# Four of eight ternary weight pieces moved from ScalarE and VectorE to GpSimd

## The reference

```python
def step(carry, xs):                    # 128 of these, one after the other
    r, state = carry
    qt, kt, vt = xs
    r = decay * r + kt * vt
    retained = (qt * r).reshape(B, D)
    inp = retained @ Wi.T + bi
    gate = sigmoid(inp @ Wg.T + bg)
    blended = gate * state + (1.0 - gate) * inp
    state = tanh(blended @ A.T + inp @ Bm.T)
    return (r, state), state @ Wo.T + bo

def _quantize(W):                       # W1 is 1024 x 256, W2 is 256 x 1024
    gamma = mean(abs(W))
    return clip(round(W / (gamma + EPS)), -1.0, 1.0)

x = x + tanh(g_xattn) * mixer(layernorm(x), ctx)
h = relu(layernorm(x) @ _quantize(W1).T + b1)
x = x + tanh(g_ffn) * (h @ _quantize(W2).T + b2)
```

## Time and profile before

| what | value |
| --- | --- |
| median of 3 runs | 324.25 us |
| lowest and highest run | 324.06 and 325.9 us |
| the profiled execution | 325.28 us |
| span of the profiled execution | 323.2 us |
| mean granted TensorE clock | 0.993 |
| TensorE busy | 307.6 us, 95% of the span |
| VectorE busy | 284.7 us, 88% |
| ScalarE busy | 237.0 us, 73% |
| GpSimd busy | 78.6 us, 24% |

### The profile page before, as it was taken

How to read it: one execution, slowest core, us unless ns; L and a number is a source line. 1 busy time by engine, 2 the same in 40 slices (tenths; PEclk the granted TensorE clock), 3 DMA queues, 4 the chain that set the end, 5 groups by cost and what they waited for, 6 DMA issues and landing times. The chain is left out here.

```text
span 323.2 us, 10197 instructions
## 1 busy us (share of the span) xinstructions
PE 307.6 (95%) x3821; PEld 280.4 (87%) x3821; DVE 284.7 (88%) x816; ACT 237.0 (73%) x556; POOL 78.6 (24%) x138
## 2 busy tenths in 40 slices
PE   6889979999999999999999999999999999999995
PEld 4677858899999999999999999999999999997784
DVE  5889897999999999999999999999999998977763
ACT  4585556787778688787877786887877777847684
POOL 2021133242131323141311313231413112141230
PEclk9999997999999999999999999999999999999999
DMA  8903414214344435151443434350514324161321
GB/s 288 393 4 99 98 34 67 65 41 61 132 68 130 69 98 101 42 126 27 137 58 130 65 130 65 104 90 32 136 26 138 57 65 65 68 99 36 67 32 65
DMA packets 19399, 29.16 MB, mean 90 GB/s; under 512 B 1840, under 2 KB 10288, under 8 KB 19120
## 3 DMA queue, kind: packets, MB, share of 16 engines
q0 software_dynamic: 8720, 8.39, 18.2%
q1 hardware_dynamic: 10224, 19.93, 17.9%
q10 hardware_dynamic: 432, 0.53, 0.5%
HBM read 16.26 MB, written 4.19 MB: 63 GB/s over the span
## 5 line engine op out<-in xcount | busy, mean ns | idle before, releaser
L467 ACT ACTIVATE state<-pre_ps,sc 128x64 f32<-128x64 f32 x128 | 40.1, 313 | 57.1 <-PE pre_ps L1053 56.8
L457 ACT ACTIVATE hid<-hid_ps,b_s 128x256 f32<-128x256 f32 x120 | 50.3, 471 | 11.5 <-PE hid_ps L1092 9.7
L1092 PE MATMUL hid_ps<-xt_lo,w_q 128*128 128x256 f16 x240 | 55.5, 272 | 0.0
L1104 PE MATMUL y_ps<-w_q,h_lo 128*128 128x256 bf16 x240 | 55.5, 272 | 0.0
L1092 PE MATMUL hid_ps<-xt_hi,w_q 128*128 128x256 f16 x240 | 55.5, 272 | 0.0
L1104 PE MATMUL y_ps<-w_q,h_hi 128*128 128x256 bf16 x240 | 55.5, 272 | 0.0
L1047 PE MATMUL pre_ps<-m_hi,a_hi 128*128 128x32 f16 x508 | 42.6, 178 | 3.7 <-DVE m_hi L681 3.7
L732 DVE TENSOR_TENSOR h_lo<-hid,h_hi 128x512 f16<-128x512 f32 x60 | 41.3, 688 | 3.6 <-ACT h_hi L463 1.4
L1047 PEld LDWEIGHTS pre_ps<-m_hi,a_hi 128*128 128x128 f16 x508 | 33.9, 96 | 9.5 <-DVE m_hi L681 5.6
L1047 PE MATMUL pre_ps<-m_hi,a_lo 128*128 128x32 f16 x508 | 41.5, 176 | 0.0
L463 ACT CAST h_hi<-hid 128x512 f16<-128x512 f32 x60 | 37.1, 619 | 1.9
(11 more groups left out here) (181 smaller groups left out, 965.7 us busy)
## 6 DMA issues: line engine op xcount, KB each, us to landing
x_norm<-x_in SPq DMA_DIRECT2D x16, 256.0 KB, 2.8
cx<-ctx_in SPq DMA_DIRECT2D x16, 256.0 KB, 3.1
x_res<-x_in SPq DMA_DIRECT2D x16, 256.0 KB, 3.4
x_res<-bo_g POOLq DMA_DIRECT2D x16, 256.0 KB, 4.8
x<-b_g POOLq DMA_DIRECT2D x15, 256.0 KB, 3.9
y_out<-y SPq DMA_DIRECT2D x15, 256.0 KB, 2.0
w_raw<-w_in SPq DMA_DIRECT2D x2, 1024.0 KB, 8.8
wsq<-wsq_in SPq DMA_DIRECT2D x3, 256.0 KB, 5.4
```

The lines of the kernel that those rows point to most:

```text
L457: last = nc.scalar.activation(hid[:, p % 2, u, :], hid_ps[p % 2][:, u * N:(u + 1) * N], ACT.Relu, bias=b1_s[:, 2 * p + u:2 * p + u + 1], s ...
L467: nc.scalar.activation(state[:, q[1] % 2, :, step_cols(j)], pre_ps[q[1] % 2][:, :].rearrange("p (k n) -> p k n", k=K)[:, :, step_cols(j)], ...
L1092: last = nc.tensor.matmul(hid_ps[p % 2][:, u * N:(u + 1) * N], w1_q[:, k, cut], v[:, par, k, :], start=n == 0, stop=n == len(terms) - 1)
L1104: last = nc.tensor.matmul(y_ps[:, t * D:(t + 1) * D], h[:, f, t * P:(t + 1) * P], w2_q[:, f, :], start=f == 0 and t == 0 and h is h_hi, st ...
```

## The change

Pieces 1, 3, 4 and 5 are made on GpSimd. For each it writes `above = w > thr` and `below = w < -thr` (128 x 512, float32) and then `above - below` into the quarter, with a wait for `below` before the difference. Piece 1 stands in GpSimd's body 0 after the reciprocal root; piece 3 at the start of body 1, piece 4 after the second reciprocal root of body 1, piece 5 at that body's end, behind both its DMAs. VectorE makes one more small value, `thr_n = -thr`, with a wait for its end, in `threshold`. Pieces 0, 2, 6 and 7 stay with ScalarE and VectorE; the signs of 6 and 7 now stand in the places that those of 4 and 5 had, after steps 2 and 4 of body 1, and their merges stay where they were. TensorE waits for GpSimd's semaphore for the four pieces, in the same places as before.

```diff
--- before.py
+++ after.py
@@ -89,7 +89,8 @@
         gate_sc = sb("gate_sc", [P, 2])
         gsum = sb("gsum", [P, 4])
         gpart = sb("gpart", [P, 2])
-        thr = sb("thr", [P, 2])
+        thr, thr_n = sb("thr", [P, 2]), sb("thr_n", [P, 2])
+        above, below = sb("above", [P, F * D // 4]), sb("below", [P, F * D // 4])
 
         x_norm = sb("x_norm", [P, 2, TILES, D])
         x_res = sb("x_res", [P, 2, TILES, D])
@@ -145,6 +146,7 @@
         idle_set = sem("idle_set")
         dve_prep = sem("dve_prep")
         act_prep = sem("act_prep")
+        below_set, ternary_set = sem("below_set"), sem("ternary_set")
         pe_prep = sem("pe_prep")
         stats1, mean1, vare1, rstd1, xh1_set = (sem(n) for n in ("stats1", "mean1", "vare1", "rstd1", "xh1_set"))
         squared, r_carried, r_set = sem("squared"), sem("r_carried"), sem("r_set")
@@ -218,8 +220,9 @@
             return tuple(plus(c, d) if exists(plus(c, d)) else None for d in (2, 1, 0, -1, -2))
 
 
-        SIGN_AT = {(0, 3): 0, (0, 5): 2, (0, 7): 1, (1, 0): 3, (1, 2): 4, (1, 4): 5, (1, 6): 6, (1, 7): 7}
-        TERNARY_AT = {(0, 4): 0, (0, 6): 2, (1, 1): 1, (1, 3): 3, (1, 5): 4, (2, 0): 5, (2, 1): 6, (2, 3): 7}
+        SIGN_AT = {(0, 3): 0, (0, 5): 2, (1, 2): 6, (1, 4): 7}
+        TERNARY_AT = {(0, 4): 0, (0, 6): 2, (2, 1): 6, (2, 3): 7}
+        POOLED = (1, 3, 4, 5)
         CHUNK, NEXT_CHUNK, THIRD = (0, 0), (0, 1), (0, 2)
         HIDDEN_SLOTS = (0, 1, 2, 4)
         LAST, NEXT = (0, NC - 1), (0, NC - 2)
@@ -244,7 +247,7 @@
 
         QUARTERS = 4
         PREP = ["zero", "keep", "wi_lo", "mx", "wg_lo", "mx_t", "mx_d", "bound", "top", "inv", "s_a", "sc", "bm_lo", "aw_lo",
-                "a_lo", "gpart", "gmean", "thr", "wo_lo", "ternary0", "ternary2", "gates_out"]
+                "a_lo", "gpart", "gmean", "thr", "thr_n", "wo_lo", "ternary0", "ternary2", "gates_out"]
         PREP += [f"ternary{n}" for slot, n in TERNARY_AT.items() if slot > (0, 6)]
         done = {name: n + 1 for n, name in enumerate(PREP)}
         APREP = ["gates", "wi", "wg", "bm", "aw", "a", "sums", "wo"]
@@ -328,16 +331,34 @@
                 pool.wait_ge(rstd1, upto(q))
                 nc.gpsimd.tensor_tensor(shift1[:, :], off1[:, :], rs1[:, :], ALU.mult).then_inc(shifted1, 1)
 
+            def ternary(n):
+
+                w, piece = n // QUARTERS, n % QUARTERS
+                raw = quarter((w1_raw, w2_raw)[w], piece)
+                pool.wait_ge(dve_prep, done["thr_n"])
+                pool.wait_ge(w1_in_s if w == 0 else w2_in_s, 16)
+                if POOLED.index(n):
+                    pool.wait_ge(ternary_set, POOLED.index(n))
+                nc.gpsimd.tensor_scalar(above[:, :], raw, thr[:, w:w + 1], None, ALU.is_gt)
+                nc.gpsimd.tensor_scalar(below[:, :], raw, thr_n[:, w:w + 1], None, ALU.is_lt).then_inc(below_set, 1)
+                pool.wait_ge(below_set, POOLED.index(n) + 1)
+                nc.gpsimd.tensor_tensor(quarter((w1_q, w2_q)[w], piece), above[:, :], below[:, :],
+                                        ALU.subtract).then_inc(ternary_set, 1)
+
             rstd1_of((0, 0))
             rstd1_of((0, 1))
 
             def body(c):
                 norm, project, chain, attend, ffn = stages(c)
                 peeled = c[1] if isinstance(c[0], int) else None
+                if peeled == 1:
+                    ternary(3)
                 if norm:
                     rstd1_of(norm)
                     if peeled != 0:
                         shift1_of(norm)
+                if peeled == 0:
+                    ternary(1)
                 if peeled == NC - 1:
                     pool.wait_ge(x_res_in[PAR], landed(LAST))
                     pool.dma_start(x_res[:, PAR, :, :], bo_g[:, :].unsqueeze(1).to_broadcast([P, TILES, D]),
@@ -350,6 +371,8 @@
                     nc.gpsimd.tensor_tensor(ve2[:, :], mv2[:, :, 1], eps[:, :], ALU.add).then_inc(vare2, 1)
                     pool.wait_ge(vare2, upto(attend))
                     nc.gpsimd.tensor_tensor(rs2[:, :], ve2[:, :], minus_half[:, :], ALU.pow).then_inc(rstd2, 1)
+                    if peeled == 1:
+                        ternary(4)
 
                     pool.wait_ge(const_set, 5)
                     pool.wait_ge(xh2_set, upto(attend))
@@ -363,6 +386,8 @@
                         pool.wait_ge(x_res_in[chain[1] % 2], landed(chain))
                     pool.dma_start(x_res[:, chain[1] % 2, :, :], bo_g[:, :].unsqueeze(1).to_broadcast([P, TILES, D]),
                                    accum_op=ALU.add).then_inc(bo_added[chain[1] % 2], 16)
+                if peeled == 1:
+                    ternary(5)
 
             run(pool, body)
 
@@ -545,7 +570,6 @@
                 rest_high(NEXT_CHUNK)
                 carry(NEXT_CHUNK)
                 square(THIRD)
-                side_sign(1)
 
             def body(c):
                 norm, project, chain, attend, ffn = stages(c)
@@ -874,6 +898,7 @@
                 prep("gmean", nc.vector.tensor_scalar(thr[:, :], y_ps[:, 0:2], 1.0 / (F * P * D), Q_EPS,
                                                       ALU.mult, ALU.add))
                 prep("thr", nc.vector.tensor_scalar(thr[:, :], thr[:, :], 0.5, None, ALU.mult))
+                prep("thr_n", nc.vector.tensor_scalar(thr_n[:, :], thr[:, :], -1.0, None, ALU.mult))
 
             def ternary(n):
 
@@ -1213,7 +1238,8 @@
                         step(chain, j)
                     if ffn and j < PAIRS:
                         if peeled == 2 and j in (0, 2):
-                            pe.wait_ge(dve_prep, done[f"ternary{(2, 3)[j // 2]}"])
+                            pe.wait_ge(dve_prep, done["ternary2"])
+                            pe.wait_ge(ternary_set, POOLED.index((1, 3)[j // 2]) + 1)
                         hidden_product(ffn, j)
                     if j == 0 and project:
                         normed_t(project)
@@ -1225,14 +1251,16 @@
                         inp_product(project)
                     if j == 4 and ffn:
                         if peeled == 2:
-                            pe.wait_ge(dve_prep, done[f"ternary{QUARTERS + 1}"])
+                            pe.wait_ge(ternary_set, POOLED.index(QUARTERS + 1) + 1)
                         y_product(ffn, 2)
                         y_product(ffn, 3)
                     if j == 4 and project:
                         gate_product(project)
                     if ffn:
                         for f in {3: (0, 1), 5: (4, 5), 6: (6, 7)}.get(j, ()):
-                            if peeled == 2 and f % 2 == 0:
+                            if peeled == 2 and f == 0:
+                                pe.wait_ge(ternary_set, POOLED.index(QUARTERS) + 1)
+                            if peeled == 2 and f in (4, 6):
                                 pe.wait_ge(dve_prep, done[f"ternary{QUARTERS + f // 2}"])
                             y_product(ffn, f)
                     if j == 5 and attend:
```

## The result

The changed kernel takes 329.73 us (329.4 to 330.36, 4 runs), against 324.62 for the kernel before (324.06 to 325.9, 4 runs): a ratio of 1.0154, with an interval of 1.0117 to 1.0191. That is 5.1 us slower. The forecast was 326.6, in a range of 322.9 to 329.3. The profiled execution took 329.41 us, with a span of 327.3.

A forecast was written before the change was run, and what follows sets the result against it. Dependent steps through chunk 1 set the pace, then TensorE; VectorE held by GpSimd at the shared memory decides. 0.2 + 1.0 + 0.3 - 0.3 + 0.2 + 1.0 = +2.4 on 324.25 gave 326.6 us, range 322.9 to 329.3.

The forecast's parts named there:

- rival D: VectorE and GpSimd hold each other for whole instructions in the dense places: +5.6 us, 329.9 us; chance 0.20.
- piece 1: VectorE's full queue at 31 to 34 us: two-input rows held, one-input scalings run on; 0.6 to 2.2, taken 1.0 us.
- GpSimd's price: Each 128 x 512 comparison 0.6 us, the difference 1.05; about 2.2 a piece, at most 1.2 an operation, 3.6 a piece.
- Piece 3: From 35.8 us, GpSimd holds VectorE's rest_lo on the path: 0 to 0.6 us, taken 0.3.
- Piece 4: Near 47.5 us, GpSimd holds VectorE's inp_lo on the path, with slack behind it: 0 to 0.6 us, taken 0.2.
- Piece 5: At 52.4 to 55 us, two-input VectorE rows held on the path to from_rest of chunk 2: 0.5 to 1.7, taken 1.0.
- A: The forecast's own sum, VectorE held part of the time: +2.4 us, 326.6 us, range 325.0 to 328.3; chance 0.50.
- The clock: TensorE's half-speed stretch in 40 to 60 us, costing up to 1.7 us, left as it is in the sum.
- The gain before step 2: In chunk 1, the merge of piece 1 gone ends TensorE's idle: 0.55 us gained, 0.3 of it then eaten by holds.
- Signs at 0: Signs leaving ScalarE give no time by themselves; at the end of body 1 VectorE's own queue ends later: 0 us.
- thr_n: One more tiny VectorE operation and its wait, on the path to from_rest of chunk 1: bounds 0 and 0.2, taken 0.2 us.
- GpSimd's queue and DMAs: The pieces and the DMAs behind them on GpSimd's queue are ready before they are wanted: 0 us.

The follow-up runs named there:

- z3: Kernel before with only piece 1 on GpSimd, plus thr_n; signs and merges of pieces 3, 4 and 5 as before; 328.41 us, ratio 1.0106.
- x1: Changed kernel without its twelve GpSimd operations, the four quarters only blanked by early GpSimd memsets; 326.89 us, ratio 1.0071.
- x3: Changed kernel with memsets of like length in place of the twelve GpSimd operations, quarters blanked early; 331.37 us, ratio 1.0217.
- y2: Changed kernel with one GpSimd operation per piece, a difference of the raw weights with themselves, and no comparisons; 329.27 us, ratio 1.0169.
- z1: y2 with the GpSimd difference of piece 3 moved ahead of the bias DMA of body 0; 328.99 us, ratio 1.014.
- x4: Changed kernel with piece 1 back on ScalarE and VectorE at its places of before; 328.5 us, ratio 1.0145.
- y1: Changed kernel without its twelve GpSimd operations, the four quarters only blanked by GpSimd memsets near 10 us; 324.88 us, ratio 1.0018.
- x5: Kernel before with VectorE's merge of piece 1 moved behind that of piece 4, after step 5 of chunk 1; 323.84 us, ratio 0.9985.
- x0: Kernel before with thr_n alone added, one tiny VectorE operation and its wait, used by nobody; 325.76 us, ratio 1.0028.
- z2: Kernel before with the merge of piece 1 and signs 1, 6 and 7 moved to other places, nothing new on GpSimd; 323.93 us, ratio 0.9983.
- y3: Changed kernel with the two GpSimd comparisons of each piece and no difference; 329.1 us, ratio 1.0149.

## Why the prediction was wrong

The measured time is 0.4 us above the range and 0.2 below the time of rival D. That GpSimd's pieces hold VectorE's two-input rows, and where, was on the page; that one-input rows are held too was not, and most terms were too small.

- **The step that failed**: piece 1, "the norm (`xh`) and five small scalings have one and run on". It took 1.6 us out of the hold of 2.2, for a lower bound of 0.6 and a term of 1.0. They don't run on. `xh` and `b_s` were held for 0.62 and 1.06 us, and `m_hi`, the only two-input row held there, for 0.37; the term measured 2.05 (2.08 by the tanh of (0,7), 2.0 to 2.9 by the runs of z3). The one-input hold is on the Trainium skill's page too (SBUF — State Buffer, "Who interferes with whom": VectorE in a two-port performance mode and GpSimd exclude each other); x1 and x3 agree, with 2.05 and 3.38 us on `xh`, if these rows run in such a mode. The profile doesn't name it. They are cheap for their length: in x3 the scalings `b_s` and `b_g` took 0.21 us for 8 columns and 0.34 for 256, by estimate 0.5 ns per column, and two-input rows 0.22 for 64 and 0.69 for 512, by estimate 1.05. I had read that section for its two-input rule only.
- **GpSimd's price**: a comparison 0.6, bounds up to 1.2; measured 1.57 to 1.66. The difference 1.05; measured 1.26 in the change and 1.04 in y2. The outcome of the comparison's error was small, since a VectorE instruction caught by one waited 0.29 to 0.80 us, not 1.57: by luck the piece's hold of 2.2 was near the 2.05, and with it D's time. The Trainium skill's lock (same section) lasts for the whole instruction. That is not what these rows show for the comparison; the difference comes nearer, with two-input rows held for 0.72 to 0.84 us by one of 1.03 to 1.31 that had started just before (y2, z1).
- **Piece 3**: `rest_lo` 0.3; measured 0.41, and 0.4 by the chain of x4. **Piece 4**: `inp_lo` 0.2, with slack behind it; `inp_lo` was held for 0.43, `xh` and the `m_hi` of step 5 behind it for 0.29 and 0.33, and the chain lost 0.9. **Piece 5**: 1.0; 0.88 to (2,0), and 0.46 more behind it, on `s_lo`. The places were right, each sum too small.
- **The range**: A was given as 325.0 to 328.3 "from the bounds at each place", but these add up to 0.2 + 2.2 + 0.6 - 0.3 + 0.6 + 1.7 = 5.0, or 329.3 us. So it was narrower than its own bounds.
- **The clock**: kept as it was in the sum. It did not stay: the stretch moved to 37 to 42 us, cost 1.2 us there, and gave 1.2 back from (1,4) to (1,5). In the profiled execution that cancels; in the runs it is 0.4 to 0.9 us.
- **The gain before step 2**: 0.55, then 0.3. From (1,0) to (1,4) it was 0.94 in the change and 1.34 in y1, more than foreseen; yet x5 gained only 0.2 to 0.3 in like clock, and y1 nothing. That such a lead isn't kept is one reading; the other is that `thr_n` in y1 eats it, by the 1.0 us of x0's runs.
- **Signs at 0**: z2 says no, for its places. ScalarE's relief, with x5's merge, was worth 0.5 to 1.0 us, and x5 alone 0.2 to 0.3.
- **thr_n**: 0.2; 0.14 in the change and 0.2 in x0 by the chain, but 1.0 by the runs of x0, which is open.
- **Right**: GpSimd's queue and DMAs cost nothing by being late, TensorE never waited for a piece, and the bodies from chunk 2 on keep their pace.

## What to carry to other kernels

Before elementwise work goes to an idle GpSimd, look at what VectorE runs beside it: here two-input instructions were held by GpSimd's reads (0.3 to 0.8 us, and 2.09 behind a DMA's issue), float32 scalings with one SBUF input by its writes (up to 2.65), and in a full queue on the path the whole hold was lost (2.05 in rows, 2.08 in the chain), whatever GpSimd's own share of busy time says. Here the bound is a chain of short steps, and moving pieces to idle places on the engines that have them was the better move (z2). Compare times at like clock when effects are under 2 us.

## What was not expected of the hardware

- A VectorE scaling of 128 x 8 took 1.28 instead of 0.22 us beside a GpSimd difference.
- A GpSimd comparison of 128 x 512 takes 1.57 us, more than the two-input difference (1.26). Four of the five two-input VectorE rows held beside one in the changed kernel waited 0.37 to 0.43 us, one 0.80; others beside one weren't held.
- The other way round, a GpSimd difference took 2.32 instead of 1.26 us when a two-input scan on VectorE had started 0.1 us before it.
- A GpSimd read placed right behind the issue of a DMA on the same engine held a VectorE row for 2.09 us; ahead of the DMA it held one for 0.84. This is one pair of runs, and the way it works isn't shown.
- The two kinds of GpSimd operation don't add up: each alone cost 5.0 to 5.1 us by the medians, and both together 5.1; at 0.994 and 0.995, against 325.0, y3 cost 3.6 to 4.1, y2 4.3 (once 6.0), and the changed kernel 4.7. The two groups of pieces nearly do in like clock: 2.4 and 2.9 to 3.6 us, and 4.2 to 4.7 together.
